# Four edits to a fused decoder kernel: order of the first transfers, rows split for the context, norms spread in half-array products, unread products in the cross-attentions

## The reference, cut to what matters

```python
qk = einsum('bthd,bshd->bhts', q, k) * scale
a = where(causal, qk ** 2 * exp(logG_t - logG_s), 0)
norm = sum(a, axis=-1) + 1e-6
y = einsum('bhts,bshd->bthd', a, v) / norm
out = y @ Wc + bc
```

## Time and profile before

| what | before |
|---|---|
| median of 3 runs (lowest, highest) | 1696.13 us (1692.6, 1697.54) |
| profiled execution's own time | 1697.4 us |
| its span, first to last instruction | 1695.6 us |
| busy: PE, DVE, ScalarE, GpSimd | 97%, 66%, 44%, 15% of the span |
| mean granted TensorE clock | 0.985 |
| chain that ended last | PE 87%, DVE 5%, DMA 3%, ScalarE 2%, GpSimd 1% |
| transfers | 71.1 MB |

### The profile page before, as it was taken

How to read it: one execution, slowest core, us unless ns; L and a number is a source line. 1 busy time by engine, 2 the same in 40 slices (tenths; PEclk the granted TensorE clock), 3 DMA queues, 4 the chain that set the end, 5 groups by cost and what they waited for, 6 DMA issues and landing times.

```text
span 1695.6 us, 35593 instructions
## 1 busy us (share of the span) xinstructions
PE 1639.0 (97%) x15222; PEld 1114.4 (66%) x15222; DVE 1112.7 (66%) x1961; ACT 746.7 (44%) x1282; POOL 246.9 (15%) x432
## 2 busy tenths in 40 slices
PE   8999999999999899999999999999999999999998
PEld 4586367777755666655367777764566757777765
DVE  2734789999566753256889999535454279999632
ACT  2223366666412542134366666312444266666411
POOL 0021200000010312011300000020465000000030
PEclk9999999999999999999999999999999899999999
DMA  5322010000040011051020000050300220000010
GB/s 204 102 67 81 1 76 2 2 2 2 2 184 1 2 58 40 1 117 61 1 95 2 2 3 2 2 238 1 63 1 1 112 88 2 2 2 2 2 44 11
DMA packets 35422, 71.10 MB, mean 42 GB/s; under 512 B 25259, under 2 KB 29675, under 8 KB 31333
## 3 DMA queue, kind: packets, MB, share of 16 engines
q1 hardware_dynamic: 35266, 68.83, 12.2%
HBM read 68.36 MB, written 0.46 MB: 41 GB/s over the span
## 4 chain that ended last, share of the span: by engine, by line
PE 87%; DVE 5%; DMA 3%; ACT 2%; issue 1%; POOL 1%; SPq 0%; ACTq 0%; DVEq 0%; POOLq 0%
PE ps L1077 14%; PE ps L1090 13%; PE ps L993 13%; PE ps L337 9%; PE ps L1444 9%; PE ps L904 3%; PE ps L2501 3%; DMA arena<-in_ctx_sin 3%; PE ps L1105 3%; PE ps L1885 2%; PE ps L914 1%; PE ps L484 1%; PE ps L2528 1%; PE ps L975 1%; PE ps L940 1%
## 5 line engine op out<-in xcount | busy, mean ns | idle before, releaser
L1186 ACT ACTIVATE arena<-ps,softmax_stats 128x1500 f32<-128x1500 f32 x168 | 254.0, 1512 | 196.7 <-DVE softmax_stats L1267 194.7
L1090 PEld LDWEIGHTS ps<-arena,ctx_pos 125*64 125x64 f32 x4608 | 222.3, 137 | 58.4 <-issue 57.6
L1077 PE MATMUL ps<-ident,arena 64*125 64x64 f32 x4032 | 240.8, 272 | 6.4 <-ACT arena L1186 6.4
L1077 PEld LDWEIGHTS ps<-ident,arena 64*125 64x125 f32 x4032 | 229.1, 187 | 21.7 <-issue 13.8
L1090 PE MATMUL ps<-arena,ctx_pos 125*64 125x128 f32 (+1 forms) x4608 | 240.5, 262 | 0.0
L993 PE MATMUL ps<-ctx_feat,arena 64*128 64x500 f32 x1008 | 234.6, 599 | 0.0
L1193 ACT COPY arena<-ps 125x512 f32<-125x512 f32 x336 | 172.5, 599 | 79.3 <-PE ps L1077 79.3
L1265 DVE TENSOR_REDUCE softmax_stats<-ps 128x1 f32<-128x500 f32 x252 | 170.7, 679 | 53.4 <-PE ps L993 53.4
L337 PE MATMUL ps<-arena 128*128 128x256 f32 x736 | 174.4, 383 | 3.5 <-ACT arena L2596 1.0
L1278 DVE TENSOR_SCALAR arena<-arena,softmax_stats 128x1500 f32<-128x1500 f32 x168 | 168.3, 1002 | 5.9
L1444 PE MATMUL ps<-x_feat,arena 128*128 128x448 f32 (+1 forms) x416 | 167.9, 549 | 1.2 <-DVE arena L1545 1.2
(11 more groups left out here) (310 smaller groups left out, 1941.6 us busy)
## 6 DMA issues: line engine op xcount, KB each, us to landing
ctx_pos<-in_ctx SPq DMA_DIRECT2D x1, 3000.0 KB
arena<-in_L1f_gate SPq DMA_DIRECT2D x1, 2304.0 KB, 12.4
arena<-in_L1f_up SPq DMA_DIRECT2D x1, 2304.0 KB, 17.4
arena<-in_L1f_down SPq DMA_DIRECT2D x1, 2304.0 KB, 7.8
arena<-in_L0a_Wq SPq DMA_DIRECT2D x1, 2048.0 KB, 10.4
arena<-in_L0a_Wc SPq DMA_DIRECT2D x1, 2048.0 KB, 11.0
arena<-in_L0x_Wq SPq DMA_DIRECT2D x1, 2048.0 KB, 10.0
arena<-in_L0x_Wo SPq DMA_DIRECT2D x1, 2048.0 KB, 8.1
```

The source lines that it names most:

```text
L1077: m = nc.tensor.transpose(c.ps[0:LP, turn_bank(i, k, r), n * 64:(n + 1) * 64], probs[i % 2][e][rows, l * LP:(l + 1) * LP], c.ident[rows, r ...
L1090: m = nc.tensor.matmul(y[r * 64:(r + 1) * 64, lo:hi], c.ctx_pos[:, j, l, e, :], pT[i % 2][:, lo // 64:hi // 64, LT * e + l, :], start=(l = ...
L1186: nc.scalar.activation(probs[i % 2][e].rearrange("p (k l) -> p k l", k=3), sc[e], ACT.Exp, bias=low[:, i % 4, e:e + 1], accum_out=total[:, ...
```

## The change

It has four parts. (1) The group `L0_start` keeps Wg and x_feat, in this order; Wk and the two tables become a group `L0_keys`, for which PE waits behind the gate products and DVE ahead of `masked`. (2) Every load whose name begins with ctx (the context and its two tables, 125 rows each) is issued as rows 0 to 111 and rows 112 to 124. (3) In the first attention the weights `a` are laid out with 64 columns per query head, the last 8 of them zero, so that the sums of query head r come out in rows 64 r on; one GpSimd operation lays the inverse norms on two 56-wide diagonals (`ident2`), and `spread` is two products of 64 rows, one in each half of the rows, r for the query head. ScalarE's copies, the division and the waits follow that layout; GpSimd has four more small operations ahead of the loop. (4) Unread products: in layer 3's front, 512 columns at t = 2 and 256 at t = 3; in all three unit loops, 512 and 256 columns at i = 1, behind the scores and a wait for ScalarE's fourth `cm` copy (line 1175, third of its own).

```diff
@@ load @@
+            if name[:3] == "ctx":
+                halves = [(dst[n], self.dram[name][n]) for n in (slice(0, 112), slice(112, LP))]
             for to, src in halves:
                 eng.dma_start(to, src).then_inc(self.loaded[group].handle, 16)
                 self.loaded[group].n += 16
@@ L0_LOADS @@
-    return [("L0_start", [("x_feat", flat(c.x_feat[:])), ("L0a_Wk", c.at(4096, 2048)), ("L0a_Wg", c.at(12288, 16)),
-                          ("L0a_after", c.at(12304, 128)), ("L0a_tri", c.at(12688, T))]),
+    return [("L0_start", [("L0a_Wg", c.at(12288, 16)), ("x_feat", flat(c.x_feat[:]))]),
+            ("L0_keys", [("L0a_Wk", c.at(4096, 2048)), ("L0a_after", c.at(12304, 128)), ("L0a_tri", c.at(12688, T))]),
@@ l0_attention, tiles @@
-    a = [c.at(33152 + 448 * i, NT) for i in range(2)]
+    a = [c.at(o, J * 2 * TP).rearrange("p (j r t) -> p j r t", j=J, r=2) for o in (33152, 29568)]
     yT = [c.at(34048 + 1024 * i, 1024).rearrange("p (r b t) -> p r b t", r=2, b=B) for i in range(2)]
-    rnorm = c.at(36096, 896).rearrange("p (h n) -> p h n", h=2)
-    ones = c.at(37088, 128, 2 * T)
-    rsum = c.at(37216, 8, 2 * T).rearrange("p (j h) -> p j h", j=J)
-    diag = [c.at(28672 + 896 * i, 896, 2 * T).rearrange("p (h j n) -> p h j n", h=2, j=J) for i in range(2)]
+    rnorm = c.at(36096, 896).rearrange("p (r n) -> p r n", r=2)
+    ones = c.at(37088, 128)
+    rsum = c.at(37216, 8).rearrange("p (j h) -> p j h", j=J)
+    ident2 = c.at(33664, T)
+    diag = [c.at(28672 + NT * i, NT) for i in range(2)]
@@ l0_attention, gpsimd @@
+        nc.gpsimd.memset(a[0][:, :, :, T:TP], 0.0).then_inc(*padded.next())
+        pool.wait_ge(c.loaded["L0_rest"].handle, c.loaded["L0_rest"].n)
+        pool.wait_ge(padded.handle, padded.at(5))
+        for r in range(2):
+            rows = slice(r * TP, (r + 1) * TP)
+            nc.gpsimd.tensor_copy(ident2[rows], c.ident[rows, r * TP:r * TP + T]).then_inc(*padded.next())
         pool.wait_ge(diffs.handle, diffs.at(2))
-        pool.wait_ge(c.loaded["L0_rest"].handle, c.loaded["L0_rest"].n)
+        pool.wait_ge(padded.handle, padded.at(7))
+        nc.gpsimd.memset(a[1][:, :, :, T:TP], 0.0).then_inc(*padded.next())
+        pool.wait_ge(padded.handle, padded.at(8))
...
-            for h in range(2):
-                nc.gpsimd.tensor_tensor(diag[g % 2][:, h], c.ident[0:2 * T, 0:2 * T].unsqueeze(1).broadcast_to([2 * T, J, 2 * T]),
-                                        rsum[:, :, h].unsqueeze(2).broadcast_to([2 * T, J, 2 * T]), ALU.mult).then_inc(*diag_in.next())
+            nc.gpsimd.tensor_tensor(diag[g % 2].rearrange("p (h j t) -> p h j t", h=2, j=J),
+                                    ident2.unsqueeze(1).unsqueeze(1).broadcast_to([128, 2, J, T]),
+                                    rsum.rearrange("p j h -> p h j").unsqueeze(3).broadcast_to([128, 2, J, T]),
+                                    ALU.mult).then_inc(*diag_in.next())
@@ l0_attention, tensor, ahead of the loop over banks @@
+        pe.wait_ge(c.loaded["L0_keys"].handle, c.loaded["L0_keys"].n)
...
-        pe.wait_ge(padded.handle, padded.at(4))
+        pe.wait_ge(padded.handle, padded.at(8))
@@ sums @@
-                m = nc.tensor.matmul(c.ps[0:2 * T, 6 + g % 2, NT + 2 * j:NT + 2 * j + 2],
-                                     a[g % 2][:, j * 2 * T:(j + 1) * 2 * T], half[:, :, 0], start=True, stop=True)
+                m = nc.tensor.matmul(c.ps[:, 6 + g % 2, NT + 2 * j:NT + 2 * j + 2],
+                                     a[g % 2][:, j].rearrange("p r t -> p (r t)"), half[:, :, 0], start=True, stop=True)
@@ spread @@
-            for h in range(2):
-                pe.wait_ge(diag_in.handle, diag_in.at(2 * g + h + 1))
-                if g > 0:
-                    pe.wait_ge(rn_in.handle, rn_in.at(2 * g - 1 + h))
-                m = nc.tensor.matmul(c.ps[:, 4 + h, 0:NT], ones, diag[g % 2][:, h], start=True, stop=True)
+            pe.wait_ge(diag_in.handle, diag_in.at(g + 1))
+            if g > 0:
+                pe.wait_ge(rn_in.handle, rn_in.at(2 * g))
+            for r in range(2):
+                rows = slice(r * TP, (r + 1) * TP)
+                m = nc.tensor.matmul(c.ps[:, 4 + r, 0:NT], ones[rows], diag[g % 2][rows], start=True, stop=True)
             m.then_inc(*spread_mm.next())
@@ weigh @@
-                                     a[g % 2][h * TP:h * TP + T, j * 2 * T:(j + 1) * 2 * T], start=True, stop=True)
+                                     a[g % 2][h * TP:h * TP + T, j, :, 0:T], start=True, stop=True)
@@ l0_attention, scalar, loop over g @@
-            for h in range(2):
-                if g > 0:
-                    act.wait_ge(y_in.handle, y_in.at(2 * g - 1 + h))
-                nc.scalar.copy(rnorm[:, h], c.ps[:, 4 + h, 0:NT]).then_inc(*rn_in.next())
+            if g > 0:
+                act.wait_ge(y_in.handle, y_in.at(2 * g))
+            for r in range(2):
+                nc.scalar.copy(rnorm[:, r], c.ps[:, 4 + r, 0:NT]).then_inc(*rn_in.next())
@@ l0_attention, vector, ahead of masked @@
+        dve.wait_ge(c.loaded["L0_keys"].handle, c.loaded["L0_keys"].n)
@@ weights @@
-            nc.vector.tensor_tensor(a[g % 2].rearrange("p (j r t) -> p j r t", j=J, r=2),
+            nc.vector.tensor_tensor(a[g % 2][:, :, :, 0:T],
@@ invert @@
-                dve.wait_ge(diag_in.handle, diag_in.at(2 * g))
...
-            nc.vector.tensor_scalar(r, c.ps[0:2 * T, 6 + g % 2, NT:NT + 8], 1e-6, None, ALU.add).then_inc(*s.dve_chain.next())
+            nc.vector.tensor_scalar(r, c.ps[:, 6 + g % 2, NT:NT + 8], 1e-6, None, ALU.add).then_inc(*s.dve_chain.next())
@@ divide @@
+            dve.wait_ge(rn_in.handle, rn_in.at(2 * g + 2))
             for h in range(2):
-                dve.wait_ge(rn_in.handle, rn_in.at(2 * g + h + 1))
                 nc.vector.tensor_tensor(
                     yT[g % 2].rearrange("p r (j h) t -> p h j r t", h=2)[:, h, :, :, 0:T],
                     c.ps[:, 2 + h, 0:NT].rearrange("p (j r t) -> p j r t", j=J, r=2),
-                    rnorm[:, h].rearrange("p (j r t) -> p j r t", j=J, r=2), ALU.mult).then_inc(*y_in.next())
-        dve.wait_ge(padded.handle, padded.at(4))
+                    rnorm.rearrange("p r (h j t) -> p h j r t", h=2, j=J)[:, h], ALU.mult).then_inc(*y_in.next())
+        dve.wait_ge(padded.handle, padded.at(8))
@@ cross_attention, tensor, front of the form without rope, loop over t @@
@@ -1038,6 +1053,9 @@
                     keep_busy(c, 4, 1)
                 if t == 2:
                     arrived("_next")
+                    keep_busy(c, 5, 1)
+                if t == 3:
+                    keep_busy(c, 5, 1, None, 256)
@@ cross_attention, tensor, loop over units @@
         for i in range(1, NU):
             for k in range(3):
                 score(i, k)
+            if i == 1:
+                pe.wait_ge(cm_act.handle, cm_act.at(3))
+                keep_busy(c, 6, 1)
+                keep_busy(c, 6, 1, None, 256)
```

More of the change, by code:

```diff
@@ L446, in _ @@
         nc.gpsimd.memset(ones, 1.0).then_inc(*padded.next())
-        pool.wait_ge(padded.handle, padded.at(4))
+        nc.gpsimd.memset(a[0][:, :, :, T:TP], 0.0).then_inc(*padded.next())
[4 more added lines that the diff above has]
+            nc.gpsimd.tensor_copy(ident2[rows], c.ident[rows, r * TP:r * TP + T]).then_inc(*padded.next())
         pool.wait_ge(diffs.handle, diffs.at(2))
-        pool.wait_ge(c.loaded["L0_rest"].handle, c.loaded["L0_rest"].n)
+        pool.wait_ge(padded.handle, padded.at(7))
+        nc.gpsimd.memset(a[1][:, :, :, T:TP], 0.0).then_inc(*padded.next())
+        pool.wait_ge(padded.handle, padded.at(8))
         for g in range(GH):
@@ L669, in invert @@
             if g > 0:
-                dve.wait_ge(diag_in.handle, diag_in.at(2 * g))
+                dve.wait_ge(diag_in.handle, diag_in.at(g))
             r = rsum.rearrange("p j h -> p (j h)")
-            nc.vector.tensor_scalar(r, c.ps[0:2 * T, 6 + g % 2, NT:NT + 8], 1e-6, None, ALU.add).then_inc(*s.dve_chain.next())
+            nc.vector.tensor_scalar(r, c.ps[:, 6 + g % 2, NT:NT + 8], 1e-6, None, ALU.add).then_inc(*s.dve_chain.next())
             dve.wait_ge(s.dve_chain.handle, s.dve_chain.last())
```

## The result

Before: median 1694.37 us over 4 runs (1692.56 to 1697.54). After: 1683.21 us over 4 runs (1679.92 to 1685.71). Ratio 0.9931, 95% interval 0.9906 to 0.9956. The profiled execution of after took 1683.76 us, span 1682.0.

The account below looks back on a forecast made before the run. TensorE, busy 97% of the span, was taken as the bound. Terms 2.6 + 2.3 + 1.7 + 4.3 + 5.5 + 3.8 = 20.2 us off 1697.4 gave 1677 us; range 1670 to 1688.

Parts of the forecast that it names:

- My own test: Wrong if the first attention ends less than 9 us earlier, or the long half-clock stretch is still there.
- Baseline: Gains subtracted from the profiled execution's 1697.4 us, taken as 1.3 above the median of 1696.1.
- Start, 2.6: First transfers: gate products run while the keys' group lands, so key products start 2.6 us earlier; bounds 0 to 3.4.
- Context, 2.3 + 1.7: First attention: split rows land the context early, saving PE's 2.3 us wait and 1.7 us of clock fall; bounds 0, 4.0.
- by 27: Transfers of the first attention: the split context and tables, 3.75 MB at 300 GB/s, land by 27 us.
- Spread, 4.3: First attention's head groups: two half-array products overlap, 0.85 instead of 1.51 us, sums 0.1 longer; 4.3 us gained.
- groups 0 and 1: First two head groups: 0.9 and 0.25 us gained within the spread's term, less 0.2 for wider sums.
- The drain: Spread: tiling-mode changes drain the engine; at most 0.11 us each, 16 take 1.8 us, making the sum 1679, not 1677.
- rival (d): First attention's loop: with the spread halved, the clock falls and stays at half; 1700 to 1734 us, chance 0.02.
- Last front, 5.5: Last cross-attention's front: unread products costing 1.3 us prevent a 13.7 us half-clock stretch; net 5.5 us gained.
- Rival (a): Cross-attentions: the unread products do not hold the clock; 1688 us, chance 0.12.
- Loop entries, 3.8: Three cross-attentions' loop entries: unread products fill 1.3 of 2.3 us idle, crediting 55% of 6.85 us lost: 3.8 us.

Follow-up runs that it names:

- e2: The kernel before with only the spread in half-array products and its layouts; median 1691.74 us, ratio 0.9990 to before.
- e3: The kernel before with only the cross-attentions' unread products (last front and loop entries); median 1687.08 us, ratio 0.9967 to before.
- e1: The kernel before with only the new order of the first transfers and the context's rows split; median 1690.52 us, ratio 0.9977 to before.
- e6: The kernel after without the split: context and its tables again one 125-row transfer each; median 1685.87 us, ratio 0.9943 to before.
- e11: The kernel after with unread products of 512 and 512 columns instead of 512 and 256 at each loop entry; median 1674.88 us, ratio 0.9878 to before.
- e7: The kernel after with each group's spread moved between the next turn's sums and the weighing; median 1681.02 us, ratio 0.9933 to before.
- e4: The kernel after with the spread as it was before; median 1686.56 us, ratio 0.9953 to before.
- e8: The kernel after without the two unread products in the last cross-attention's front; median 1687.53 us, ratio 0.9954 to before.
- e9: The kernel after without the unread products at the three loop entries; median 1688.99 us, ratio 0.9949 to before.

## Why the prediction was right or wrong

Faster was right, and 1683.21 lies in the range, 6 us above 1677. That the sum comes this close is in part luck: the terms below miss on both sides, and the clock's own draws are as large as the terms. My own test was missed: I had said I was wrong if the first attention ended less than 9 us earlier, and it ended 5.0 earlier. (A slip in the range: the bounds at their best add up to 25 us, not 24.) Term by term:

- **Baseline.** I set the sum against one execution at 1697.4 us, called 1.3 above the median. Over 30 later runs before's median was 1693.81, so it lay 3.6 above. It had drawn a late context: with the same transfers, e2 and e3 landed it 2 us earlier, PE waited 0.9 us at most and no fall followed.
- **Start, 2.6.** The keys start 2.1 us earlier in after, 2.5 in e1 and e6 (at 8.3), but I took it for granted that a lead at the start is a lead at the end. It is worth 1.0 in after, where full speed came at 14.9 us as in before. Full speed came at 11.1 to 15.8 us in the 14 profiles; e1, at 12.7, ended the first 32 key records at 22.75, 2.3 us ahead of before, and e11, at 11.1, at 21.89, 3.2 ahead. So the term is right within what the clock adds or takes. x_feat landed at 4.8 and the gate products ended at 8.4, as worked out; but the keys' last table landed at 8.67, not 7.4, and PE waited 0.3 us for it. Why only there, I do not know.
- **Context, 2.3 + 1.7.** The mechanism holds (e6 against after and e1). The first sums come 5.3 us earlier (81.95 to 76.66), 4.3 of it from here, against 4.0. Against a usual execution the term was oversized: e1 as a whole gained 3.3 us of median (1693.81 to 1690.52), where start and context stood at 6.6. The share of 0.90 in after's window of 20 to 27, against 0.34, shows that the context uses more engines. The rule of the Trainium skill ("DMA: Bandwidth & Descriptors", section "Why a DMA increments its semaphore by 16 and not by 1") has 112 rows on 16 engines, which agrees. But the 300 GB/s that I took for it was wrong: those engines moved 162 GB/s, where the fewer ones of the earlier trace rows moved 141. My landing "by 27" was missed by it. After's transfers from 0 to 60 us, in 40 slices of 1.5 us:

```profile
GB/s 0 109 388 399 441 414 404 513 257 213 213 262 246 197 246 238 43 131 225 257 259 351 369 458 418 448 231 44 0 0 0 0 0 0 0 0 0 0 0 0
```

  Its first 18 slices, up to 27 us, make 7.1 MB, and all transfers up to the context are 7.6 MB. The values' weights, queued behind the context, land at 35.1 (6.94 + 28.2), and DVE starts on the context at 41.2 without a wait, so the error cost nothing.
- **Spread, 4.3.** This step failed. "I take 0.85, for changes of the array's shape on both sides" and the sums' "0.1 longer" priced the pair alone. Before's chain has 1.51 for the spread and 0.69 for the sums (98.67 to 99.37); after's has 0.95 and 0.98, the rest of the turn alike. So 0.56 is gained where I had 0.66, and 0.29 lost where I had 0.1: 0.27 net a turn, not 0.56, 1.6 over the six turns where I had 3.4; the rest of the measured 2.64, 1.0, is groups 0 and 1, as forecast. e7 shows why: its sums take 0.79, so the wider stationary costs the 0.1 that I gave it, and the other 0.19 is the change of row layout, behind which the weight load no longer runs ahead. The weighing, 1.08 before and after, becomes 0.88 once the spread stands ahead of it. The drain that I had weighed from the Trainium skill ("TensorEngine Tiling", "Key Properties") was the right objection, though what the rows show is only that no weight load runs ahead; I had let talk it down to 0.11 us, and its 1679 was the better sum.
- **Groups 0 and 1.** In after the loop took 66.2 us (76.66 to 142.83), 0.3 more than before: the 2.64 were paid back by the half-clock stretch of 6.8 us. That is a fall where rival (d) had put it, at a small size, in the very groups that I gave as evidence against it. That the spread brings it is not shown: the old one fell in 1 of 4 profiles, the new one in 4 of 7, and both start the loop at another moment than before. With e2 at 0.9990 and e4 3.4 us above after, whose intervals overlap, part three's own worth in the median stays between nothing and about 3 us; the counts above make it 0.8 (2.64 less 1.8).
- **Last front, 5.5.** Right: it held, and the last cross-attention gained 6.6 us with its entry. Rival (a) is real at a lesser rate (e4). In a mean execution the products are worth 4.0 us by the counts, and e8's median, 4.3 above after, agrees without being clear of the noise.
- **Loop entries, 3.8.** I credited 55% because the fillers take that share of the idle time; 13 of 24 entries held. No run shows that the one share sets the other, so the match is luck. In after two held and the second did not, which gave 5.1 us; the counts make it 4.1 in a mean execution. e9, 5.8 us above after, and e11, 8.3 below, carry more than the entries alone: e9's loop over the groups took 4.6 us more than after's, and the entries can give e11 no more than 2.3 in the mean. The windows at the entries agree; where the rest of e11's 8.3 comes from is open.
- **Elsewhere.** A stretch at 605.4 is new in after, and one at 554.2 moved to 547.4. Work there is unchanged. The one near 605 is also in e1, e4, e6 and e11, so it is another draw: 1.7 us.

In sum, the span gained 13.6 of 20.2 us. Of the 6.6 missing, 1.7 is the spread's price, 2.9 the fall in groups 0 and 1, 1.3 start (1.6 short) and context (0.3 more), and 0.7 the cross-attentions with all else: 8.6 us gained behind the first attention (13.6 less 5.0) where front and entries stood at 9.3.

## What to carry to other kernels

When a reordering shrinks two operations, price their neighbours too: put products of one row layout next to each other. Where TensorE's clock falls in a thin stretch, full-length unread products in its waits can be worth several times their cost (4.0 us net for 1.3 in the front, by the counts), and making them longer (512 + 512 for 512 + 256) ended the falls at the entries. Price a saving ahead of the first full-speed product at what is left behind it: 2.1 us became 1.0. Take the baseline from many runs and count falls over many profiles: one profile's stall and clock fall may be its own.

## What the runs showed of the hardware

- A stretch at half clock lasted up to 17.1 us with PE busy for all of it (e9's and e4's windows above), and the same code fell or held from one kernel to the next.
- At the loop entries PE was busy for 4.62 to 4.69 of the 7.0 us before e9's three falls; with 6.37 one entry of after held and one fell.
- TensorE ran its first products at half speed, and the first record of full clock began at 11.1 (e11) to 15.8 us (e2), 14.9 in before and after.
- With the 112 + 13 rows the transfer engines had a busy share of 0.90 and moved 162 GB/s (after, 20 to 27 us); with 125 rows it was 0.34 and 141 GB/s (before, 28 to 34 us).
- Eight weight loads of 128 columns with two-column products cost 0.79 us behind a product of the same 128 rows (e7) and 0.98 behind 64-row products (after, e2).
- Unchanged 125-row transfers landed 2 us apart (46.2, 46.5, 48.5 us) in kernels whose starts are alike; in e6, issued at 4.37, the last table took 43.9 us.
- Left open: what decides, in the stretches that sometimes fall, whether they do, and when the first full clock comes. No run was made to tell that.
